# Cross-attention and LoRA-MoE feed-forward on one core: eight slots for x, x loaded five tiles ahead, the store behind the small transfers, and the first norm's statistics at the step's end

## The reference

```python
# first half: attention over the 64 context rows
scores = einsum('bsd,bmd->bsm', layernorm(x), ctx) / sqrt(D)
attn = softmax(where(mask, scores, -1e30))
x = x + einsum('bsm,bmd->bsd', attn, ctx)       # zero where no row is valid
# second half: dense layer plus two of eight LoRA experts
y = layernorm(x)
base = einsum('btd,od->bto', y, weight)
probs = softmax(einsum('btd,ed->bte', y, router_w)); top 2, renormalised -> w_dense
Ax = einsum('nd,erd->ner', y, lora_A)
expert_out = einsum('ner,ne,eor->no', Ax, w_dense, lora_B) * 2.0
x = x + base + expert_out
```

## Time and profile before

| What | Before |
|---|---|
| median of 3 runs | 1057.44 us (1056.31 to 1058.38) |
| the profiled execution | 1056.82 us |
| its span, first to last instruction | 1055.0 us |
| PE, PE weight loads, DVE, ACT, POOL busy | 99%, 97%, 78%, 45%, 10% |
| granted TensorE clock | 1.00 in every stretch after the start |
| DMA moved | 156.8 MB, 149 GB/s |

### The profile page before, as it was taken

The page is one execution under the profiler, slowest core; times in us unless marked ns, Lnnn a source line. Parts: engine busy times, 40 slices in busy tenths (PEclk is TensorE's granted clock), DMA queues, the critical chain, the costliest instruction groups (busy, mean ns, idle before and its releaser), DMA issues.

```text
span 1055.0 us, 18697 instructions
## 1 busy us (share of the span) xinstructions
PE 1045.1 (99%) x6078; PEld 1027.3 (97%) x6078; DVE 823.2 (78%) x2203; ACT 478.2 (45%) x929; POOL 103.6 (10%) x278
## 2 busy tenths in 40 slices
PE   8999999999999999999999999999999999999998
PEld 7999999999999999999999999999999999999998
DVE  6967877887878878878777888778787778787773
ACT  7744543535434445435445345444354354354330
POOL 3200101101001001001011010010010110110100
PEclk9999999999999999999999999999999999999999
DMA  8464566665467555665656665665656655555532
GB/s 311 161 178 118 159 144 149 187 133 130 132 167 182 134 121 155 160 162 157 141 119 182 152 149 131 141 174 133 159 150 144 146 158 145 148 152 115 112 79 75
DMA packets 157247, 156.81 MB, mean 149 GB/s; under 512 B 95120, under 2 KB 130064, under 8 KB 157200
## 3 DMA queue, kind: packets, MB, share of 16 engines
q1 hardware_dynamic: 139056, 152.85, 54.0%
q10 hardware_dynamic: 18144, 3.42, 3.2%
HBM read 78.74 MB, written 33.55 MB: 106 GB/s over the span
## 4 chain that ended last, share of the span: by engine, by line
PE 82%; DVE 7%; SPq 4%; DMA 2%; ACT 2%; issue 1%; POOL 1%; ACTq 0%; DVEq 0%; POOLq 0%
PE base_ps L1053 24%; PE base_ps L1054 24%; PE base_ps L1055 24%; PE s_ps L1080 3%; PE ro_ps L1117 2%; PE s_ps L1081 2%; PE ro_ps L1118 2%; SPq L367 2%; DVE x L857 1%; DVE stats L863 1%; SPq L394 1%; SPq L330 1%; DMA h<-w_raw 1%; ACT xn L578 1%; DVE xT_lo L882 1%
## 5 line engine op out<-in xcount | busy, mean ns | idle before, releaser
L1053 PE MATMUL base_ps<-w_hi,xT_hi 128*128 128x388 f32 x1512 | 513.6, 340 | 0.0
L1054 PE MATMUL base_ps<-w_lo,xT_hi 128*128 128x388 f32 x1512 | 511.7, 338 | 0.0
L1055 PE MATMUL base_ps<-w_hi,xT_lo 128*128 128x388 f32 x1512 | 511.2, 338 | 0.0
L1054 PEld LDWEIGHTS base_ps<-w_lo,xT_hi 128*128 128x128 f32 x1512 | 284.6, 188 | 2.6
L1053 PEld LDWEIGHTS base_ps<-w_hi,xT_hi 128*128 128x128 f32 x1512 | 283.9, 188 | 2.7
L1055 PEld LDWEIGHTS base_ps<-w_hi,xT_lo 128*128 128x128 f32 x1512 | 284.2, 188 | 0.0
L875 DVE STREAM_TRANSPOSE x2T<-xq 128x512 f32<-128x512 f32 x122 | 124.2, 1097 | 74.2 <-DMA xq<-xn 74.1
L559 ACT CAST eT<-w_raw 128x128 fp32r<-128x128 f32 x60 | 18.0, 300 | 266.8 <-DMA w_raw<-w_raw 266.8
L468 POOL TENSOR_TENSOR rstd<-var_eps,neg_half 128x1 f32<-128x1 f32 x64 | 35.1, 548 | 880.1 <-DVE var_eps L868 880.1
L578 ACT ACTIVATE xn<-x,shift,rstd 128x1024 f32<-128x1024 f32 x61 | 75.9, 1244 | 71.7 <-POOL shift L471 71.6
L857 DVE SCALAR_TENSOR_TENSOR x<-ro_ps,e_scale,x 128x512 f32<-128x512 f32 x128 | 89.9, 745 | 1.9 <-PE ro_ps L1118 1.8
(11 more groups left out here) (120 smaller groups left out, 1121.2 us busy)
## 6 DMA issues: line engine op xcount, KB each, us to landing
out<-x SPq DMA_DIRECT2D x63, 512.0 KB, 2.9
xT_raw<-in_xT SPq DMA_DIRECT2D x62, 512.0 KB, 5.4
x<-in_x SPq DMA_DIRECT2D x62, 512.0 KB, 3.6
xq<-xn SPq DMA_DIRECT2D x244, 128.0 KB, 3.7
h<-w_raw SPq DMA_DIRECT2D x248, 16.0 KB, 1.9
w_raw<-w_raw SPq DMA_DIRECT2D x120, 32.0 KB, 1.9
ctx_raw<-in_ctx SPq DMA_DIRECT2D x7, 520.0 KB, 3.4
w_raw<-in_wT SPq DMA_DIRECT2D x8, 386.0 KB, 8.5
```

Of the source, the lines that this page charges most:

```text
L1053: pe.matmul(out_, a_hi, w_h, start=start, stop=False, skip_group_check=again)
L1054: pe.matmul(out_, a_hi, w_l, start=False, stop=False, skip_group_check=again)
L1055: return pe.matmul(out_, a_lo, w_h, start=False, stop=stop, skip_group_check=again)
```

## The change

x gets eight slots instead of four. Slots 0 to 3 are a buffer of their own (`x_first`), slots 4 to 7 lie in the space of the raw weights, which is free once the weights have been split. The load of x is issued five tiles ahead (`XA`) instead of four, and waits for the store of the tile three before, not for the one just issued. On SP the store of a step comes behind the exchanges of `xn`, `e`, `h` and, in even steps, of the scores; the context of the next batch is loaded at the end of step 1 of a batch, not of step 0. On ACT, `norm1` of tile t+3 stands at the end of step t instead of at the head of step t+1. On POOL, `norm1` of t+3 stands ahead of `norm2` of t+2. The hunks left out only write `x(tile)` for `x[:, slot(tile), :]`.

```diff
--- before.py
+++ after.py
@@ -54,7 +54,9 @@
     TPB = NT // NB
     CW = ctx_in.shape[2]
     T2 = 2 * P
-    XS = 4
+    XS = 8
+    XF = 4
+    XA = 5
     Q = 4
     QP = P // Q
     DQ = D // Q
@@ -131,7 +133,7 @@
         mask_bias = sb("mask_bias", [P, M])
         any_valid = sb("any_valid", [P, 1])
 
-        x = sb("x", [P, XS, D])
+        x_first = sb("x_first", [P, XF, D])
         xn = sb("xn", [P, D])
         xq = sb("xq", [P, Q, DQ])
         xT_raw = sb("xT_raw", [P, 2, 2, C, P])
@@ -180,6 +182,10 @@
         hT_hi = sb("hT_hi", [P, P], f32r)
         hT_lo = sb("hT_lo", [P, P], f32r)
 
+
+        x_rest = [w_raw[0], w_raw[1], w_raw[1], w_raw[1]]
+        x_from = [0, 0, D, 2 * D]
+
         hq = w_raw[0][:, C - 1, 0:P]
         eq = w_raw[0][:, C - 1, P:2 * P]
         e_raw = w_raw[0][:, C - 1, 2 * P:3 * P]
@@ -195,6 +201,13 @@
 
         st_ps = ro_ps[:, 0:2 * M]
         et_ps = ro_ps[:, H:H + P]
+
+        def x(tile):
+
+            i = slot(tile) - XF
+            if i < 0:
+                return x_first[:, slot(tile), :]
+            return x_rest[i][:, :, :].rearrange("p c n -> p (c n)")[:, x_from[i]:x_from[i] + D]
 
         def base_bank(tile, g):
             return base_ps[g][tile[1] % len(base_ps[g])]
...
@@ -358,7 +371,7 @@
             def store(tile):
                 b, j = tile
                 sp.wait_ge(out_done, count(tile, G, FREE + G))
-                sp.dma_start(out[b * TPB + j], x[:, slot(tile), :]).then_inc(stored[slot(tile)], 16)
+                sp.dma_start(out[b * TPB + j], x(tile)).then_inc(stored[slot(tile)], 16)
 
             def exchange(tile):
 
@@ -369,10 +382,10 @@
 
             sp.dma_start(ctxT_raw[:, 0:HC, :], ctxT_in[0][:, 0:HC, :]).then_inc(ctxT_loaded, 16)
             sp.dma_start(xT_raw[:, 0, 0, 0:HC, :], xT_in[0][:, 0:HC, :]).then_inc(xT_loaded[0][0], 16)
-            sp.dma_start(x[:, 0, 0:H], x_in[0][:, 0:H]).then_inc(x_loaded[0], 16)
+            sp.dma_start(x((0, 0))[:, 0:H], x_in[0][:, 0:H]).then_inc(x_loaded[0], 16)
             sp.dma_start(ctx_raw[:, 0:H], ctx_in[0][:, 0:H]).then_inc(ctx_loaded, 16)
             sp.dma_start(xT_raw[:, 0, 1, 0:HC, :], xT_in[1][:, 0:HC, :]).then_inc(xT_loaded[0][1], 16)
-            sp.dma_start(x[:, 1, 0:H], x_in[1][:, 0:H]).then_inc(x_loaded[1], 16)
+            sp.dma_start(x((0, 1))[:, 0:H], x_in[1][:, 0:H]).then_inc(x_loaded[1], 16)
             for g in range(2):
                 for r in range(WPARTS):
                     load_w(g, r)
@@ -386,6 +399,9 @@
                 sp.wait_ge(w_split[1][r], 1)
             sp.dma_start(b_raw, bT_in).then_inc(b_loaded, 16)
             load_xT((0, 4))
+            for r in range(2):
+                sp.wait_ge(w_split[2][r], 1)
+            load_x((0, 4))
 
             def h_exchange(tile):
 
@@ -403,26 +419,30 @@
             def step(tile, first=False):
 
                 b, j = tile
-                store(tile)
                 if exists(after(tile, 2)) and not first:
                     exchange(after(tile, 2))
                 if exists(after(tile, 3)) and not first:
                     e_exchange(sp, after(tile, 3), 2)
                 if exists(after(tile, 1)) and not first:
                     h_exchange(after(tile, 1))
-                if exists(after(tile, XS)):
-
-                    sp.wait_ge(stored[slot(tile)], b * (16 * TPB // XS) + 16 * (j // XS + 1))
-                    load_x(after(tile, XS))
+                if j % 2 == 0 and exists(after(tile, 4)) and not first:
+                    s_exchange(after(tile, 4))
+                store(tile)
+                if exists(after(tile, XA)):
+                    bx, jx = after(tile, XA)
+                    if not isinstance(b, int) or b > 0 or jx >= XS:
+                        sp.wait_ge(stored[jx % XS], b * (16 * TPB // XS) + 16 * (jx // XS))
+                    elif jx == XF + 1:
+                        sp.wait_ge(b_split, 1)
+                    load_x(after(tile, XA))
                 if first:
                     sp.wait_ge(xT_split, pairs((0, 2), 2, 2))
                     load_xT((0, 6))
+                    s_exchange(after(tile, 4))
                 if j % 2 == 1 and exists(after(tile, 7)):
                     sp.wait_ge(xT_split, pairs(after(tile, 3), 2, 2))
                     load_xT(after(tile, 7))
-                if j % 2 == 0 and exists(after(tile, 4)):
-                    s_exchange(after(tile, 4))
-                if j == 0 and exists((b, TPB)):
+                if j == 1 and exists((b, TPB)):
                     sp.wait_ge(ctx_split, b + 1)
                     sp.wait_ge(mask_step, b * 3 + 3)
                     load_ctx(b + 1)
@@ -439,7 +459,7 @@
             for g in range(G):
                 o0, n = OUTS[g]
                 sp.wait_ge(out_done, count(LAST, G, FREE + g + 1))
-                sp.dma_start(out[NT - 1][:, o0:o0 + n], x[:, slot(LAST), o0:o0 + n]).then_inc(stored[slot(LAST)], 16)
+                sp.dma_start(out[NT - 1][:, o0:o0 + n], x(LAST)[:, o0:o0 + n]).then_inc(stored[slot(LAST)], 16)
             for s in range(XS):
                 sp.wait_ge(stored[s], 16 * NT // XS + (16 * (G - 1) if s == slot(LAST) else 0))
 
@@ -471,8 +491,9 @@
                 pool.tensor_tensor(shift2[:, :], neg_mean2[:, :], rstd2[:, :], ALU.mult).then_inc(shift2_done, 1)
 
             def step(tile):
+                if exists(after(tile, 3)):
+                    norm1(after(tile, 3))
                 if exists(after(tile, 2)):
-                    norm1(after(tile, 2))
                     norm2(after(tile, 2))
 
             norm1((0, 0))
@@ -492,6 +513,7 @@
             norm1((0, 3))
             norm2((0, 2))
             norm2((0, 3))
+            norm1((0, 4))
             for j in range(2, TPB):
                 step((0, j))
             with pool.Fori(1, NB - 1) as b:
...
@@ -631,9 +653,6 @@
             def step(tile):
                 b, j = tile
                 nxt, nxt2 = after(tile, 1), after(tile, 2)
-                if exists(nxt2):
-                    norm1_mean(nxt2)
-                    norm1_squares(nxt2)
                 if exists(nxt):
                     norm2(nxt)
                 if exists(nxt2):
@@ -653,13 +672,16 @@
                 if j % 2 == 1 and exists(after(tile, 5)):
                     for i in range(2):
                         xT_high(after(tile, 5), i)
+                if exists(after(tile, 3)):
+                    norm1_mean(after(tile, 3))
+                    norm1_squares(after(tile, 3))
 
             act.dma_start(ctxT_raw[:, HC:C, :], ctxT_in[0][:, HC:C, :]).then_inc(ctxT_rest_loaded, 16)
             act.dma_start(xT_raw[:, 0, 0, HC:C, :], xT_in[0][:, HC:C, :]).then_inc(xT_rest_loaded[0], 16)
-            act.dma_start(x[:, 0, H:D], x_in[0][:, H:D]).then_inc(x_rest_loaded[0], 16)
+            act.dma_start(x((0, 0))[:, H:D], x_in[0][:, H:D]).then_inc(x_rest_loaded[0], 16)
             act.dma_start(ctx_raw[:, H:CW], ctx_in[0][:, H:CW]).then_inc(ctx_rest_loaded, 16)
             act.dma_start(xT_raw[:, 0, 1, HC:C, :], xT_in[1][:, HC:C, :]).then_inc(xT_rest_loaded[1], 16)
-            act.dma_start(x[:, 1, H:D], x_in[1][:, H:D]).then_inc(x_rest_loaded[1], 16)
+            act.dma_start(x((0, 1))[:, H:D], x_in[1][:, H:D]).then_inc(x_rest_loaded[1], 16)
             act.wait_ge(constants_ready, CONSTANTS)
             act.copy(gate_num[:, :], neg_half[:, :]).then_inc(tables_loaded, 1)
             xT_high((0, 0), 0)
@@ -711,6 +733,8 @@
             first_eT_copy((0, 3))
             for i in range(2):
                 xT_high((0, 6), i)
+            norm1_mean((0, 4))
+            norm1_squares((0, 4))
             for j in range(2, TPB):
                 step((0, j))
             with act.Fori(1, NB - 1) as b:
...
```

More of the change, by code:

```diff
@@ L340, in load_x @@
                 b, j = tile
-                sp.dma_start(x[:, slot(tile), :], x_in[b * TPB + j]).then_inc(x_loaded[slot(tile)], 16)
+                sp.dma_start(x(tile), x_in[b * TPB + j]).then_inc(x_loaded[slot(tile)], 16)
             def load_xT(tile):
@@ L517, in norm1_mean @@
                 b, j = tile
-                xs = x[:, slot(tile), :]
+                xs = x(tile)
                 junk = x2T[:, :, :].rearrange("p c n -> p (c n)")
@@ L577, in norm2 @@
                 act.wait_ge(x2T_done, count(tile, TS))
-                act.activation(xn[:, :], x[:, slot(tile), :], ACT.Identity, bias=shift2[:, :],
+                act.activation(xn[:, :], x(tile), ACT.Identity, bias=shift2[:, :],
                                scale=rstd2[:, :]).then_inc(xn_done, 1)
@@ L613, in first_norm2 @@
                     act.activation(half(xn, i).rearrange("p (c a n) -> p a c n", a=Q, n=QP),
-                                   x[:, slot(tile), :].rearrange("p (a c n) -> p a c n", a=Q, n=QP)[:, :, i * HC:(i + 1) * HC],
+                                   x(tile).rearrange("p (a c n) -> p a c n", a=Q, n=QP)[:, :, i * HC:(i + 1) * HC],
```

(8 more changed lines are left out.)

## The result

| What | Before | After |
|---|---|---|
| median, on the same chip in turns | 1057.84 us (4 runs) | 1072.10 us (1071.27 to 1072.60, 4 runs) |
| ratio, 95% interval | | 1.0140 (1.0128 to 1.0153) |
| the profiled execution, its span | 1056.82, 1055.0 us | 1072.00, 1070.2 us |
| PE busy | 1045.1 us, 99% | 1050.5 us, 98% |
| DMA moved | 156.8 MB | 156.8 MB |

What follows compares the result with a forecast made beforehand. It took the loop from xn to xn, as long as a PE tile, to become the bound: 1056.82 + 27 - 11 - 2 - 0.9, about 1070, then 0.6 for the median and 1 for the tail: 1071.5 us, range 1055.5 to 1079.

Steps and rivals of the forecast that it cites:

- POOL's order, 1.06 us in every second round: On POOL, norm2 behind the next tile's norm1 starts 1.06 us late where the squares end late, every second round.
- The sum on the loop, 27 us: POOL's delays over all rounds: 22 us plain, 2.5 us context steps, 2.5 us other rounds; from nothing to 61 us.
- Absorbed, 11 us: Loop time formerly spent waiting for PE takes up 11 us of the delay; ends 6 and 26.5 us.
- DVE's wait for the logits shrinks from 26.5: Sign if right: on DVE, the wait for the router's logits, 26.5 us in 33 places, gets smaller.
- The store behind the small transfers, - 2: On SP, xq and e no longer share DMA engines with a store just ahead: 2 us gained, of 0 to 8.
- The start, - 0.9: At the start, tile 5's load no longer follows a landed store; PE's first wait for eT, 0.9 us, goes.
- the tail, + 1: At the end, a loop that is the bound adds 1 us, from 16.54 against PE's 16.04 in two or three tiles.
- x earlier, nothing: ACT's waits for x, 30.4 us in 19 places, go, but nearly all were hidden behind POOL: no gain counted.
- PE as the bound: Rival: slack and DVE's waits swallow the loop's added time, leaving the start's gain: 1056.5 to 1057.5 us; chance 0.16.
- The rival of the transfers: Rival: transfers were the real limit, so moving the store and early x shorten the loop: 1054.5 us; chance 0.13.
- That of SP: Rival: SP, waiting for the scores with store and load behind, passes the next xn: 1080 to 1090 us; chance 0.05.

Runs made afterwards that it cites:

- experiment 1: Changed kernel with POOL's norm2 of t+2 put back ahead of norm1 of t+3, all else kept: 1055.37 us, ratio 0.998.
- experiment 3: Changed kernel with norm2 ahead of norm1 on POOL in odd steps only: 1055.46 us, ratio 0.9981.
- experiment 5: Changed kernel with ACT's first norm (mean and squares) ahead of the two xT casts, POOL's order as changed: 1056.86 us, ratio 1.000.
- experiment 8: Changed kernel plus a 0.55 us power on POOL: behind norm1's wait 1111.63 us, ahead of it 1079.05; with norm2 first 1062.44; spare column alone 1080.06.
- experiment 7: Changed kernel with only the store moved back to the head of SP's step: 1072.86 us, ratio 1.0145.
- experiment 2: Kernel before with only POOL's new order, norm1 of t+3 ahead of norm2 of t+2: 1086.73 us, ratio 1.0274.

## Why the prediction was right

It gave 1071.5 us, and the median was 1072.1. The mechanism held, and so did the two large terms. The store's gain did not come, and one sign on the waits was wrong.

- *POOL's order, 1.06 us in every second round.* Right: `norm2` starts 1.10 us after the variance, 0.08 before, and squares to `xn` is 1.86 us for 0.76. Experiments 1, 3 and 5 show it three ways, and the doses of experiment 8 show that it is the wait in front of `norm2`, not POOL's time.
- *The sum on the loop, 27 us, of which 24.5 in every second round and 2.5 in the others.* Right: from variance to `xn` the 59 rounds take 26.9 us more, 24.6 and 2.4 (rounded). The prediction's count was off, 21 and six rounds where it had said 29. The trace has 21 plain rounds, with 22.1 us, and eight with the late variance (tiles 4, 12, 20 and so on), with 2.5 us or some 0.3 each.
- *Absorbed, 11 us.* Near, and partly luck, since 11 was picked between 6 and 26.5 and not worked out: 26.9 - 16.5 leaves 10.4 us. They are the time that SP stood idle between `xq` and `e` (5.0 us less) and the way from `hT_hi` to the variance (6.9 us less), the latter mostly in context rounds; SP's issues and the rest take 1.4 of it back. Both come back in experiment 1, where the loop is short again: they are there when DVE's work follows PE's pace. In the round of tile 39 the router waited 1.40 us for PE; after, on DVE:

```profile
653.88 0.17 DVE L914 MAX8 top<-base_ps 128x8 f32<-128x8 f32 x1 [0.66 <-PE base_ps L1079]
```

- *SP's issues.* No term stood for them, and they matter little in the sum (+ 0.9 us), but they moved. With `rstd` early, the softmax is early, and ACT issues its half of `e` 1.32 us after SP's first `xq` instead of 1.98 (median). Before, SP's four `xq` took under 2.62 us in 56 of 61 rounds; in the changed kernel they did in 16, and took over 2.75 in 38. SP's two issues of `e`, which ACT's issues fell on before, got shorter. So two queues that issue together seem to slow each other down by up to 0.25 us; no run separates that from the rest. Where `e` was short already, as in the round of tile 33 (15.63, 15.88 after), the longer `xq` is a loss.
- *DVE's wait for the logits shrinks from 26.5.* Wrong: it is 26.8. In context rounds it fell (1.40 to 0.66 above), in the rounds of tiles 25, 33, 41, 49 and 57 it grew from about 0.4 to 0.9 or more. There SP still issues `xq` when the wait ends and goes on to `e` without idling (0.05 us at most in those of tiles 25 to 49), so it costs the loop nothing there. The total of a wait doesn't tell how much of it lies on the loop.
- *The store behind the small transfers, - 2.* Wrong: nothing. SP's issues got no shorter in sum, and experiment 7 shows no difference.
- *The start, - 0.9, and the tail, + 1.* `xn` of tile 4 starts at 77.50 instead of 78.77, 1.3 us earlier. Behind `xn` of tile 63 nothing changed (- 0.1 us); the last six rounds ahead of it, part of the 59, have 0.7 us. Together: 16.5 - 1.3 - 0.1 = 15.1 us, and the spans differ by 15.2. That the total was met within 1 us is luck to the extent that the missing - 2 of the store and the + 1 of the tail cancel in part.
- *x earlier, nothing.* Right against the kernel before, wrong as a general statement: under the new POOL order it saves 12 to 14 us (experiments 2 and 7). Without it ACT waits for x in 27 places, nearly all in odd or context rounds, where the squares then end late enough for `norm2` to start later.

Of the rivals, PE as the bound falls with experiment 1: with the loop at its old length, PE waits for `eT` only 0.6 us and the time is 1055.4. The rule of the Trainium skill that it leaned on (Perfetto Trace Analysis, Identifying the Most-Contended Engine) would have had no change; PE's weight loads were at 97% before and 96% after, while POOL at 10% set 14 us. The rival of the transfers would have been faster than before, and `xq`, at a median of 3.7 us to land in both kernels, came no sooner. That of SP falls with SP's rows: in the round shown it has issued the scores, the store and the load by 551.73, and the next `xn` only ends at 556.50.

## What to carry to other kernels

POOL's rows show that it works in the order of its program: `norm2` had its input at 553.16 and started at 554.26, behind `norm1`. So the first thing to ask of a reordering is which of the two inputs comes last. 0.8 us of work in front of a step on the critical loop costs that much, plus the wait for its input, as far as both reach beyond the step's own input: here 1.1, 0.3 or 0.1 us a round, depending on the kind of round, however idle the engine is. Put what is on the loop first, or make the other input early; either was enough here. Walk the loop against the pace of the bound engine before trusting busy shares: with a slack of 0.9 us in two plain rounds there was little room. And of parts that look worthless alone, ask whether they cover for another part of the same change.

## What was not expected of the hardware

A column of 4 bytes a partition, reserved ahead of `x_first` and never used, costs 7 to 8 us (1080.06 against 1072.10 us; ratios to before 1.0219 and 1.0140). Where it goes can be seen: the 59 rounds take 7.6 us more, and 6.1 of them lie between SP's last issue of `h` and `hT_hi`, all in six rounds near the two ends (tiles 5, 6, 9, 13, 57 and 61). These DMA rows (what, count, KB each, median us from issue to landing) are the changed kernel's and then the one with the column:

```profile
xq<-xn SPq DMA_DIRECT2D x244, 128.0 KB, 3.7
```

```profile
xq<-xn SPq DMA_DIRECT2D x244, 128.0 KB, 3.4
```

And on ACT, `hT_hi` of the last rounds, with the column and, below it, in the changed kernel:

```profile
1028.02 0.30 ACT L617 CAST hT_hi<-h 128x128 fp32r<-128x128 f32 x1 [3.41 <-DMA h<-w_raw]
```

```profile
1019.84 0.30 ACT L616 CAST hT_hi<-h 128x128 fp32r<-128x128 f32 x1 [0.99 <-DMA h<-w_raw]
```

`xq` lands sooner, but in those few rounds the last of the four `h` lands late: here 3.46 us after its issue instead of 1.87, with the store issued right behind it in both kernels (`xn` of tile 61 to `hT_hi` is 10.89 us against 9.01), and in 55 rounds out of 61 SP's `xq` issues are the long ones. Its odd rounds are 15.94 against 15.81. The Trainium skill (DMA: Bandwidth & Descriptors, How a descriptor splits into AXI transactions) has it that a descriptor which doesn't start on a 256 byte boundary costs extra beats. The rule would count if the column took buffers off such a boundary. If the buffers lie one behind another as the kernel declares them, `x_first`, and with it `xn` and `xq`, stand 68 bytes past a multiple of 256 without the column and 72 with it, so they were off in both, and the median of `xq` got shorter. So read, the rule doesn't explain the runs. Whether the buffers' place does it in some other way, or only the shifted timing, stays open; no other shift was tried. For a reader with an experiment in hand: reserve new buffers behind the existing ones, or run the reservation alone as a control.
